# A fused RWKV attention and FP4 feed-forward layer: tiles written out with four steps of lag, gate/up in three neighbouring PSUM banks, late norms on VectorE

## The reference, cut to what matters

```python
xx = concat([x[:, 1:2], x[:, :-1]], axis=1) - x      # token shift
xr, xv, xg, xk = (x + xx * mix for mix in (mix_r, mix_v, mix_g, mix_k))
r, k, v = xr @ W_r.T, xk @ W_k.T, xv @ W_v.T
g = sigmoid(xg @ W_g.T)
w = exp(-exp(time_decay))                            # per channel
# per head of 16 channels, token by token:
#   state = state * w + k v^T ;  out = state r
y = (scan(r, k, v, w) * g) @ W_o.T
y = (y - mean(y)) / sqrt(var(y) + 1e-5) * gamma + beta
x = layernorm(x + y)
def q(t):                                            # FP4, blocks of 16
    scale = max(max(abs(block)) / 6, 1e-12)
    return nearest_grid_value(t / scale) * scale     # 0 .5 1 1.5 2 3 4 6
gate, up = q(x) @ q(w_gate).T, q(x) @ q(w_up).T      # 256 -> 704
h = silu(gate) * up
x = layernorm(x + q(h) @ q(w_down).T)                # 704 -> 256
```

## Time and profile before

| what | value |
|---|---|
| median of three runs | 618.11 us |
| lowest, highest run | 615.62, 620.52 us |
| span of the profiled execution | 615.0 us |
| busy share of the span: PE, PEld, DVE, ACT, POOL | 87%, 74%, 82%, 43%, 48% |
| mean granted TensorE clock, share of 2.4 GHz | 0.962 |
| DMA | 13.13 MB, mean 21 GB/s |

### The profile page before, as it was taken

The page is one execution under the profiler, slowest core; times in us unless marked ns, Lnnn a source line. Parts: engine busy times, 40 slices in busy tenths (PEclk is TensorE's granted clock), DMA queues, the critical chain, the costliest instruction groups (busy, mean ns, idle before and its releaser), DMA issues.

```text
span 615.0 us, 14613 instructions
## 1 busy us (share of the span) xinstructions
PE 536.5 (87%) x5120; PEld 455.6 (74%) x5120; DVE 507.0 (82%) x1535; ACT 265.6 (43%) x613; POOL 292.9 (48%) x439
## 2 busy tenths in 40 slices
PE   0766788999999999999999999999999999977854
PEld 0655567788888888888888888888888887766743
DVE  2898765988899988889898888888988998786661
ACT  1444444445444444544444544554544443422211
POOL 2333523545555445555555545445555544564221
PEclk9878879999999999999999999999999999998896
DMA  7300000000000000000000000000000000000000
GB/s 188 124 1 2 10 11 10 1 19 19 18 19 19 20 18 10 10 20 19 18 19 20 19 18 18 20 18 19 18 20 10 10 10 11 10 10 9 10 9 21
DMA packets 14045, 13.13 MB, mean 21 GB/s; under 512 B 2576, under 2 KB 13712, under 8 KB 13968
## 3 DMA queue, kind: packets, MB, share of 16 engines
q1 hardware_dynamic: 13968, 12.13, 6.6%
HBM read 7.93 MB, written 4.19 MB: 20 GB/s over the span
## 4 chain that ended last, share of the span: by engine, by line
POOL 40%; issue 36%; PE 10%; DVE 10%; ACT 2%; DMA 1%; SPq 1%; POOLq 0%; DVEq 0%; ACTq 0%
POOL scores L383 11%; POOL rstd L365 8%; POOL hq L425 8%; POOL nmr L377 4%; POOL xb L412 3%; POOL xq L392 3%; DVE mix L1083 2%; POOL shift L401 2%; PE bank L896 2%; PE bank L791 2%; PE bank L771 1%; DMA x_tok<-in_L_attn_x_dram 1%; ACT scores L538 1%; PE bank L714 1%; PE bank L876 1%
## 5 line engine op out<-in xcount | busy, mean ns | idle before, releaser
L1083 DVE SCALAR_TENSOR_TENSOR mix<-shift,mu,x_t 128x128 f32<-128x128 f32 x256 | 109.1, 478 | 1.8 <-POOL shift L401 1.8
L365 POOL TENSOR_TENSOR rstd<-veps,neg_half 128x1 f32<-128x1 f32 x96 | 57.1, 605 | 92.6 <-DVE veps L1030 92.6
L538 ACT COPY scores<-bank 128x512 f32<-128x512 f32 x128 | 65.7, 600 | 62.4 <-PE bank L714 62.4
L896 PE MATMUL bank<-down_t,hq_t 128*128 128x256 f32 x384 | 90.6, 387 | 0.7 <-ACT hq_t L596 0.7
L425 POOL TENSOR_TENSOR hq<-late,h_scale 128x704 f32<-128x704 f32 x32 | 50.0, 1563 | 85.9 <-DVE late L942 85.9
L383 POOL TENSOR_SCALAR_AFFINE_SELECT scores<-scores 128x512 f32<-128x512 f32 x128 | 81.7, 670 | 4.1 <-ACT scores L538 4.1
L771 PE MATMUL bank<-gu_hi,xq_hi 128*128 128x352 f32 x256 | 68.7, 350 | 15.1 <-DVE xq_lo L1165 8.5
L896 PEld LDWEIGHTS bank<-down_t,hq_t 128*128 128x128 f32 x384 | 73.5, 194 | 10.1 <-ACT hq_t L596 1.1
L1131 DVE TENSOR_TENSOR late<-late,bank 128x352 f32<-128x352 f32 x64 | 33.0, 516 | 56.0 <-ACT late L543 56.0
L791 PE MATMUL bank<-mix,proj_t 128*128 128x128 f32 x512 | 70.7, 296 | 7.5 <-DVE mix L1083 3.4
L791 PEld LDWEIGHTS bank<-mix,proj_t 128*128 128x128 f32 x512 | 66.3, 209 | 13.6 <-issue 9.0
(11 more groups left out here) (124 smaller groups left out, 1106.5 us busy)
## 6 DMA issues: line engine op xcount, KB each, us to landing
x_tok<-in_L_attn_x_dram SPq DMA_DIRECT2D x32, 128.0 KB, 2.2
out_dram<-late_down SPq DMA_DIRECT2D x32, 128.0 KB, 1.7
late_down<-in_L_ffn_w_down_dram SPq DMA_DIRECT2D x1, 704.0 KB, 8.4
late<-in_L_ffn_w_gate_dram SPq DMA_DIRECT2D x1, 640.0 KB, 7.2
late<-in_L_ffn_w_up_dram SPq DMA_DIRECT2D x1, 640.0 KB, 7.4
scores<-in_L_attn_W_r_dram SPq DMA_DIRECT2D x1, 256.0 KB, 4.8
scores<-in_L_attn_W_v_dram SPq DMA_DIRECT2D x1, 256.0 KB, 5.2
scores<-in_L_attn_W_g_dram SPq DMA_DIRECT2D x1, 256.0 KB, 5.4
```

Source lines behind the costliest of these rows:

```text
L365: g.tensor_tensor(rstd[:, i:i + 1], veps[:, i:i + 1], neg_half, ALU.pow).then_inc((rstd_ready, x_rstd, y_rstd)[i], 1)
L538: s.copy(scores[:, t.c % 2, 4 * q:4 * q + 4, :], src).then_inc(s_moved, 1)
L896: mm = t_.matmul(B_PA[:, 0:C], hq_t[:, t.c % 2, j], down_t[:, j], start=(j == 0), stop=(j == NH - 1))
L1083: ins = v.scalar_tensor_tensor(mix[:, t0.c % 2, i, k], shift[:, t0.c % 2, k], mu[:, i, k:k + 1], x_t[:, t0.c % 2, k, 1:P + 1], ALU.mult, A ...
```

## The change

The fast path gets lists of its own (`tiles()` on every engine, over n = 0 to 35), in which a tile passes in four steps of lag: in step n, tile n is turned, mixed, projected and scored; tile n-1 gets its sums, outputs, output projection, first and second norm and the quantising of x; tile n-2 its gate and up products; tile n-3 SiLU, product, quantising and turning of the hidden values; tile n-4 the down product, the last norm and the store. 32 tiles take 36 steps.

- Gate and up are 1408 neighbouring PSUM columns, the last 384 of bank 5 and all of banks 6 and 7. 18 float32r matmuls per tile (12 of 512 columns, 6 of 384) replace 24 of 352. One SiLU and one DVE product of 704 columns replace two of 352.
- Second and third norm: one DVE instruction adds epsilon for both, one POOL instruction takes both powers, and two `tensor_scalar` instructions on DVE (L1602, L1610) do what POOL's bias product and ACT's normalising did.
- The two 64-row tails of the gate and up weights share one piece (seven pieces instead of eight). ACT's second copy (`gu_full`) is gone: DVE takes the low parts directly from PSUM.
- The first DMA is the decay vector; the gate weights, the tails, two tiles of x and the mix vectors follow, then up, gamma, beta and down. The five square weights are started from ACT's queue.

```diff
-        bank = [ctx.enter_context(nc.psum_tensor(f"bank{i}", [P, 512], F32))[:] for i in range(8)]
-        B_T, B_PA, B_PB, B_S0, B_S1, B_O, B_GATE, B_UP = bank
+        psum = ctx.enter_context(nc.psum_tensor("psum", [P, 8 * 512], F32))[:]
+        B_T, B_O, B_PA, B_PB, B_S0, B_S1, B_GATE, B_UP = (
+            psum[:, 512 * i:512 * i + 512] for i in range(8))
+        GU_0 = 8 * 512 - 2 * HID
+        gate_out, up_out = psum[:, GU_0:GU_0 + HID], psum[:, GU_0 + HID:GU_0 + 2 * HID]
...
+            def late_rstds(n):                                    # POOL
+                lo, hi = 1 if live(n - 1) else 2, 3 if live(n - DEEP) else 2
+                pool.wait_ge(eps_ready, n)
+                g.tensor_tensor(rstd[:, lo:hi], veps[:, lo:hi],
+                                neg_half.broadcast_to([P, hi - lo]), ALU.pow).then_inc(late_rstd, 1)
...
+            def tiles():                                          # POOL
+                for n in range(NT + DEEP):
+                    p = n - 1
+                    if live(n - 2):
+                        scale_x(n - 2)
+                    if live(n):
+                        difference(n)
...
+                    if live(p):
+                        add_beta(p)
+                        first_rstd(p)
+                    if n:
+                        late_rstds(n)
+                    if live(n - 3):
+                        scale_hidden(n - 3)
+                    if live(n):
+                        for i in range(QUADS):
+                            mask(n, i)
...
+            def tiles():                                          # PE
+                for n in range(NT + DEEP):
+                    p, m2, m3 = n - 1, n - 2, n - 3
...
+                    if live(p):
+                        pe.wait_ge(attn_ready, p + 1)
+                        wait(pe, hid_step, min(m2, NT))
...
+                        project_out(p % 2).then_inc(wo_done, 1)
...
+                    if live(n):
+                        pe.wait_ge(mixed, 4 * n + 4)
+                        wait(pe, s_moved, QUADS * (n - 1) + 2)
+                        project(B_PB, n % 2, G)
+                        project_k(B_PB[:, C:2 * C], n % 2).then_inc(g_k_done, 1)
...
+                    if live(m3):
+                        pe.wait_ge(hq_ready, m3 + 1)
+                        need(pe, s_moved, n, QUADS, 2)
+                        wait(pe, h_t_ready, 2 * m3)
+                        hidden_turned(m3 % 2).then_inc(h_tr, 1)
...
+            def tiles():                                          # DVE
...
+                    if live(m3):
+                        dve.wait_ge(sig_ready, m3 + 1)
+                        v.tensor_tensor(hid, sig_all, up_out, ALU.mult).then_inc(hid_step, 1)
...
+                    if n == 0:
+                        weights(0, 1)
+                        weights(2, 3)
...
+                    hstep(m3, 6)
...
+                    if live(p):
+                        dve.wait_ge(late_rstd, n)
+                        v.tensor_scalar(x1[:, p % TPB], u, mv[:, 1, 0:1], rstd[:, 1:2],
+                                        ALU.subtract, ALU.mult).then_inc(x1_done, 1)
+                    if moves:
+                        state_next(p)
+                    xstep(p, 0)
+                    if live(m4):
+                        dve.wait_ge(late_rstd, n)
+                        dve.wait_ge(y_stored[m4 % 2], 16 * (m4 // 2) + 1)
+                        v.tensor_scalar(y_out[:, m4 % 2], u2, mv[:, 2, 0:1], rstd[:, 2:3],
+                                        ALU.subtract, ALU.mult).then_inc(y_ready, 1)
+                    for k in range(1, QN):
+                        xstep(p, k)
...
+                    if n == 2:
+                        weights(5, 6)
```

More of the change, by code:

```diff
@@ L71, in tile_at, with run_tiles, live, need @@
     return tile
-def run_tiles(eng, step, looped, ahead=0, early=None):
-    def whole(tile, c=None):
-        step(tile)
-        if early and c is not None:
-            early(c)
-    for c in range(TPB):
-        whole(tile_at(0, c), c)
-    last = B - 1 if ahead else B
-    if looped:
-        with eng.Fori(1, last) as b:
-            for c in range(TPB):
-                whole(tile_at(b, c))
-    else:
-        for g in range(TPB, last * TPB):
-            whole(tile_at(g // TPB, g % TPB))
-    for c in range((B - last) * TPB + LAG_MAX):
-        whole(tile_at(last, c))
-def turn_at(stage, general):
-    return 0 if general else (2, 3, 4)[stage]
+def run_tiles(eng, step, early=None):
+    for c in range(TPB):
+        step(tile_at(0, c))
+        if early and c == 0:
+            early()
+    with eng.Fori(1, B) as b:
+        for c in range(TPB):
+            step(tile_at(b, c))
+    for c in range(LAG_MAX):
+        step(tile_at(B, c))
+def live(n):
+    return 0 <= n < NT
+def need(eng, sem, tiles, per=1, more=0):
+    wait(eng, sem, per * min(tiles, NT) + (more if tiles < NT else 0))
 def either_path(eng, flag, run):
@@ L616, in _, with run @@
+            def run(general):
+                if general:
+                    run_tiles(act, step, early)
+                else:
+                    tiles()
             act.wait_ge(flag_ready, 2)
-            either_path(act, flag, lambda general: run_tiles(
-                act, lambda tile: step(tile, general), general,
-                early=lambda c: early(c, general)))
+            either_path(act, flag, run)
         @blk.tensor
@@ L795, in project_g_k, with products @@
[L795 removed]
+                    mm = products(b[:, 0:HH], t.c % 2, o + i * HH)
+                mm.then_inc(gu_done, 1)
+            def products(dst, slot, o):
+                parts = [(x, w, k) for x, w in ((xq_hi, gu_hi), (xq_hi, gu_lo), (xq_lo, gu_hi))
+                         for k in range(KC)]
+                for n, (x, w, k) in enumerate(parts):
+                    mm = t_.matmul(dst, x[:, slot, k], w[:, k, o:o + dst.shape[1]],
+                                   start=(n == 0), stop=(n == len(parts) - 1))
+                return mm
@@ L900, in _, with run @@
+            def run(general):
+                if general:
+                    run_tiles(pe, step, early)
+                else:
+                    tiles()
             pe.wait_ge(flag_ready, 2)
-            either_path(pe, flag, lambda general: run_tiles(
-                pe, lambda tile: step(tile, general), general,
-                early=lambda c: early(c, general)))
+            either_path(pe, flag, run)
         @blk.vector
```

1057 lines of the change are left out of this document (643 added, 414 removed).

## The result

The changed kernel takes 661.89 us (median of four runs, 661.66 to 663.40) against 619.32 us for the kernel before, run beside it (615.62 to 621.23). The ratio is 1.069, with a 95% interval of 1.065 to 1.074: slower by 7%. The profiled execution spans 660.0 us. The forecast was 632.5 us and the range ended at 652. The direction and the engine were right; the size was not.

A forecast was written before the change was run, and what follows sets the result against it. PE set the pace before the change, with DVE close behind; after it DVE was to be the bound. 97 + 28 x 17.3 + 48 = 629.4, and 3.1 for profile against median: 632.5 us, range 598 to 652.

The forecast's parts named there:

- D: End of the kernel: the four rounds in which the pipeline runs empty behind tile 31's own; 48 us, bounds 44 and 53.
- PE's floor: Even round, PE's side: the shortest round PE's work allows, 16.22 us less waits of about 0.2, so 16.0 us.
- first rival: DVE's tail behind the hidden values loses under 0.8 us and PE still paces at 16.0 us; 596 us, chance 0.27.
- The collision: DVE's tail: POOL's hidden scaling holds SBUF-only DVE instructions 1.3 us, masks cost 0.8 more; round 17.3 us.
- F: Start of the kernel: the time at which tile 4 enters; 97 us, bounds 90 and 102.
- second rival: Even round: the loop from product through DVE, POOL, hidden turn, gate/up and SiLU binds at 16.7 us; 616 us, chance 0.24.
- third rival: DVE's tail waits out all four masks, 2.55 us, so a round takes 18.8 us; 650 to 674 us, chance 0.06.
- (c): Start, round 1: a chain from scores to the second four turns with their low parts, no longer bound by throughput; 19 us.
- P: Length of one even round, counted 28 times (tiles 4 to 31); 17.3 us, with DVE, not PE, as the bound.
- (a): Start: the first mix begins at about 15 us, not 17, as the decay comes first and tables end early.
- (b): Start, round 0: mixes, four weight pieces, keys, gates and four low parts on DVE; it ends at 35.5 us.
- (d): Start, round 2: like round 1 without the turns, 13 us, and 1408 columns of down weights, 8.7 us.

The follow-up runs named there:

- e3: Changed kernel with most work of two POOL steps left out (masks 8 of 128 columns, hidden scaling 16 of 704); 611.3 us.
- e18: Changed kernel with POOL's order alone swapped: it scales the hidden values before taking the late powers; 687.4 us.
- e5: e4 with the state's second decay half issued on DVE ahead of the normalising of x; 631.6 us.
- e7: Changed kernel with only the first four rounds reordered (tile 0's scores ahead of the gate weights' turns, weight pieces moved into gaps); 655.3 us.
- e17: e15 with e7's start, and DVE's wait for the decay tables moved to their first use; 617.3 us.
- e9: e5 with POOL's masks held until DVE's fifth quantising step of x, and the shift ahead of the scaling of x; 649.0 us.
- e13: e5 with masks late as in e9, but the next tile's x turned early and its shift ahead of the masks; 640.7 us.
- e12: e5 with the normalising of x and y and the x_scale step written as SCALAR_TENSOR_TENSOR with a broadcast operand; 631.5 us.
- e4: Changed kernel with the last hidden quantising step ahead of the keys, gate power later, and POOL's hidden scaling before the late powers; 632.2 us.
- e15: e5 with the last norm's normalising (y) moved from DVE to ACT; 621.6 us.

## Why the prediction was right in kind and wrong in size

**D was right in its sum** (48.3 for 48; see above for its parts). **PE's floor was right as a figure**: PE is busy 0.9688 x 16.25 = 15.7 us a round in e3, against 0.976 x 16.22 = 15.8 before, and the round without collisions is 16.25 us, inside the first rival's 16.6. The longer products did not give what was put on them, though. From start to start the 18 take 1.56 + 1.53 + 1.14 = 4.2 us in a round of e3 (310.71 to 312.27, 313.34 to 314.87 and 315.44 to 316.58), the 24 before 2.03 + 1.99 = 4.0.

**The collision was right as a mechanism**, at the predicted instruction, and DVE paces because of it, at 93 of 100 us where over 95 was written down. The first rival (no collision, 596 us) fell: e3 is what it described and gives 611 even so, 9 us of the difference in F (106.2 for 97) and 7 in the round (16.25 for 16.0). The second rival (the loop, 616 us) fell too: the product of SiLU and up starts directly behind the last step of x (307.15 + 0.42 us, then 307.49) and never waits for SiLU, and e18's earlier scaling gave nothing. The third rival, masks that hold DVE's tail whole, fell by its size: L1482 and L1160 lose 0.43 and 0.4 us, not 2.5. That 661.9 us lies in its 650 to 674 is chance: its round was 18.8 us, the measured one 17.93, and the rest is F. The Trainium skill (SBUF — State Buffer, the section on the two separate sides) speaks of a lock for a whole instruction; the runs agree for the scaling, and for the masks only if each mask of 0.64 us is taken alone. The prediction read that rule as one lock over all four, but no instruction here waits for longer than one mask. Neither reading says why y ran beside a mask unhurt here and not in e5.

**Two terms failed: F by 12.7 us, most of it in (c), and P by 28 x 0.63 = 17.6 us.** (c) is round 1 of the start, taken as a chain of 19 us. By the same marks (end of one round's low parts to the next, with weights at their own ends):

| step | predicted | measured |
|---|---|---|
| (a) first mix begins | 15 | 18.9 |
| (b) round 0, to the end of the low parts | 20.5 | 21.4 |
| (c) round 1, to the end of its low parts | 19 | 25.2 |
| (d) round 2, with the down weights | 21.7 | 22.9 |
| (e) round 3 and the clock | 20.8 | 21.3 |

(c) left out the masks of tile 0 and the fifth weight piece, and was costed as if tile 1 could be mixed once DVE is free. It can't:

```profile
40.49 2.09 PE L1036 MATMUL psum<-r_par,rv 32*128 32x256 f32 x16 [0.63 <-DVE gu_lo L1239]
42.57 2.05 ACT L699 COPY scores<-psum 128x512 f32<-128x512 f32 x4 [2.29 <-PE psum L1036]
43.23 3.00 POOL L484 TENSOR_SCALAR_AFFINE_SELECT scores<-scores 128x512 f32<-128x512 f32 x4 [5.58 <-ACT scores L699]
46.20 0.61 POOL L458 TENSOR_TENSOR shift<-x_t 128x256 f32<-128x256 f32 x1
46.85 2.39 DVE L1435 SCALAR_TENSOR_TENSOR mix<-shift,mu,x_t 128x128 f32<-128x128 f32 x4 [2.28 <-POOL shift L458]
```

The scores of tile 0 wait for the last low part (their banks are the turns' banks), the masks for the scores, and the shift of tile 1 stands behind the masks on POOL: 6.6 us from 40.27 to 46.85, of which the fifth piece fills 4.3. The prediction had 3 us for scores and copies and about 0.6 for the shift there, so this place is about 3 of the 6.2 us. The other 3 lie behind the first mixes. PE had stood idle from 30 to 36 us, and the granted clock was 0.50 from 36 to 47, 0.64 from 47 to 56 and 0.74 from 56 to 65; 1 to 2 us had been allowed for the clock in the whole start. How much of the other 3 us is the clock is not separated. e7, which moves the turns of the gate weights out of the scores' way, won 6.9 us of F. (a) took no account of DVE's wait for all tables ahead of its branch, which costs 1.3 us of the 3.9 (e17). The rest is POOL's first shift, which the new order of DMAs did not move: it runs at 16.64 us now and at 16.48 before. Its queue waits for the tables, whose last DVE instruction ends at 15.45, and for beta.

**P's terms, 17.93 for 17.3**, mis-sized in both directions. (1) The two normalisings were priced at 0.29 us by `x_mag`, an integer instruction of the same shape; they take 0.41 and 0.40, which adds 0.23. (2) The scaling was put at 1.3 us and costs x 1.06; but POOL's power is itself held by DVE's last hidden step (1.28 us, 0.70 in e18), and DVE waits 0.46 where 0.3 was put: together 0.1 less. (3) The masks were put at 0.8; state 0.43, `x_scale` 0.4, `x_grid` 0.1 and the first mix 0.14 (0.74 for 0.60, beside beta's addition) make 1.1: 0.3 more. (4) The keys wait 0.51, not 0.4. These sum to 0.5 of the 0.63; the other 0.1 I can't place. I took single prices from single collisions and left out that POOL is also slowed.

**What stays open.** Why e17's PE stood at the lower clock for longer is not settled, nor how much of its 3.5 us against e7 the clock is. Why y is held by the masks in e5 and not in the changed kernel isn't shown. Whether an order exists in which masks, shift and scalings all fall beside PSUM readers isn't shown: e9 and e13 are two tries that failed. The price of ACT's side of the first normalising (x, on the chain) was not tried.

## What to carry to other kernels

Two engines that share a way to SBUF are one resource: write down, for the stretch behind each release, which instructions of each have SBUF operands only, before you merge, delay or gather them. Reordering SBUF work among itself moved the loss here (e5, e12); other work beside it (e4) or work on a third engine (e15) took some of it away. Look also at what else such a reordering fills: in e4 it was a wait. A start that takes tiles in with fewer steps of lag must be followed queue by queue: here the shift of tile 1 stood behind tile 0's masks, and these behind the turned gate weights.

## What the runs showed of the hardware that was not expected

- POOL loses to DVE as DVE loses to POOL: a power of 128x2 took 1.28 us beside a 128x704 SCALAR_TENSOR_TENSOR and 0.70 with DVE idle beside it (e18); a 128x2 epsilon of DVE 0.57 beside the scaling and 0.17 alone.
- A DVE instruction held by masks of 0.64 us lost 0.3 to 0.46 us whatever its own size (128x16, 128x64 and 128x256 all did); `x_grid`, at the end of the last mask, lost 0.1. The reduction lost nothing beside the masks; beside the scaling the keys (which read PSUM) and the statistics lost nothing.
- `tensor_scalar` with two per-partition operands on 128x256 float32 takes 0.41 us; the integer one with constants 0.29.
